# The second MLP product of a two-layer transformer kernel as three products of scaled fp16 halves

## The reference

```python
def _layer(x, wqkv, qs, ksc, wo, lg, lb, w1, b1, w2, b2):
    h = shift_token(x)
    q, k, v = jnp.split(h @ wqkv, 3, axis=-1)
    ...
    o = local_attention(q, k, v)          # windows of 128, 8 heads of 64
    x = x + o @ wo
    h = shift_token(x)
    ...
    h = (h - mu) / jnp.sqrt(var + 1e-05) * lg + lb
    h = h @ w1 + b1
    a, g = jnp.split(h, 2, axis=-1)       # 682 features each
    h = a * jax.nn.gelu(g, approximate=False)
    return x + h @ w2 + b2
```

## Time and profile before

| | |
|---|---|
| median of 3 runs | 3270.62 us (3269.76 to 3274.61) |
| profiled execution, its own time | 3271.01 us |
| profiled execution, span | 3269.2 us |
| granted TensorE clock, mean | 0.980 of full |
| TensorE matmul busy | 3107.2 us (95%) |
| VectorE busy | 2759.7 us (84%) |
| ScalarE busy | 2013.2 us (62%) |
| GpSimd busy | 1868.5 us (57%) |
| W1 products (L950) | 4224 records, 473.2 us |
| W2 products (L961) | 1536 records, 342.2 us |

### The profile page before, as it was taken

The page is one execution under the profiler, slowest core; times in us unless marked ns, Lnnn a source line. Parts: engine busy times, 40 slices in busy tenths (PEclk is TensorE's granted clock), DMA queues, the critical chain, the costliest instruction groups (busy, mean ns, idle before and its releaser), DMA issues.

```text
span 3269.2 us, 86769 instructions
## 1 busy us (share of the span) xinstructions
PE 3107.2 (95%) x25624; PEld 2611.0 (80%) x25624; DVE 2759.7 (84%) x7865; ACT 2013.2 (62%) x4509; POOL 1868.5 (57%) x2307
## 2 busy tenths in 40 slices
PE   6999999993699999999999999999999999999997
PEld 3665748483588888888888888888888888888886
DVE  6878797976688888888888888898888898888896
ACT  5526171712367777677767777677666667667674
POOL 2333434243566566666666666666666666666673
PEclk9999999995799999999999999999999999999999
DMA  1111202026111111111111111111111111111111
GB/s 36 43 54 35 67 26 72 24 64 214 30 44 42 45 39 42 47 41 44 39 44 45 43 42 39 51 47 51 49 45 48 56 47 48 51 45 47 55 50 40
DMA packets 205471, 162.56 MB, mean 50 GB/s; under 512 B 25646, under 2 KB 203282, under 8 KB 204946
## 3 DMA queue, kind: packets, MB, share of 16 engines
q1 hardware_dynamic: 205330, 161.06, 15.9%
HBM read 106.44 MB, written 54.54 MB: 49 GB/s over the span
## 4 chain that ended last, share of the span: by engine, by line
PE 67%; issue 3%; DVE 2%; ACT 1%; POOL 1%; DMA 0%; ACTq 0%; DVEq 0%; POOLq 0%; SPq 0%
PE b_ps L874 15%; PE b_ps L950 14%; PE b_ps L961 8%; PE b_ps L902 7%; PE b_ps L890 7%; PE b_ps L915 6%; PE b_ps L929 5%; PE b_ps L859 2%; PE b_ps L852 1%; PE b_ps L841 1%; PE b_ps L827 1%; ACT L1018 1%; ACT b_probs L1018 1%; POOL b_sq L1208 0%; DVE b_probs L1169 0%
## 5 line engine op out<-in xcount | busy, mean ns | idle before, releaser
L874 PE MATMUL b_ps<-b_wqkv,b_hT_hi 128*128 128x512 f32 x1536 | 495.8, 404 | 14.6 <-DVE b_qT_low L1116 13.6
L1018 ACT ACTIVATE b_probs<-b_probs,b_negmax 128x256 f32<-128x256 f32 x1024 | 505.5, 497 | 4.1 <-DVE b_negmax L1156 3.3
L950 PE MATMUL b_ps<-b_h2T,b_w 128*128 128x256 f16 x4224 | 473.2, 273 | 0.7 <-ACT b_h2T L981 0.7
L950 PEld LDWEIGHTS b_ps<-b_h2T,b_w 128*128 128x128 f16 x4224 | 414.0, 98 | 48.7 <-ACT b_h2T L981 0.8
L1208 POOL TENSOR_TENSOR b_sq<-b_sq 128x512 f32<-128x512 f32 (+5 forms) x768 | 418.2, 545 | 60.6 <-ACT b_sq L997 20.1
L1240 POOL TENSOR_TENSOR b_rn<-b_ss_min,b_mhalf 128x16 f32<-128x16 f32 x128 | 374.8, 2928 | 119.2 <-DVE b_ss_min L1068 119.0
L1169 DVE TENSOR_SCALAR b_probs<-b_probs,b_rinv 128x256 f32<-128x256 f32 x1024 | 426.8, 458 | 18.2
L1218 POOL TENSOR_TENSOR b_rstd<-b_var,b_mhalf 128x1 f32<-128x1 f32 x128 | 72.0, 562 | 571.6 <-DVE b_var L1129 571.6
L443 PE MATMUL a_ps<-a_xs,a_E 128*128 128x256 f16 x3072 | 345.2, 273 | 4.1 <-POOL a_xs L234 4.0
L874 PEld LDWEIGHTS b_ps<-b_wqkv,b_hT_hi 128*128 128x128 f32 x1536 | 282.5, 191 | 76.5 <-DVE b_qT_low L1116 18.7
L961 PE MATMUL b_ps<-b_w,b_hid 128*128 128x256 f32 x1536 | 342.2, 379 | 1.2 <-DVE b_hid L1192 1.2
(11 more groups left out here) (137 smaller groups left out, 6653.6 us busy)
## 6 DMA issues: line engine op xcount, KB each, us to landing
b_hx<-xs_dram SPq DMA_DIRECT2D x256, 64.0 KB, 1.9
b_rot<-rot_dram SPq DMA_DIRECT2D x128, 128.0 KB, 2.1
b_xr<-xs_dram SPq DMA_DIRECT2D x128, 128.0 KB, 2.1
xp_dram<-b_xp SPq DMA_DIRECT2D x128, 128.0 KB, 1.7
b_h<-xp_dram SPq DMA_DIRECT2D x256, 64.0 KB, 1.8
a_xn<-in_L_attn_x_dram SPq DMA_DIRECT2D x20, 512.0 KB, 3.8
a_x_res<-in_L_attn_x_dram SPq DMA_DIRECT2D x66, 128.0 KB, 2.1
x_dram<-a_x SPq DMA_DIRECT2D x64, 128.0 KB, 1.7
```

Of the source, the lines that this page charges most:

```text
L874: last = nc.tensor.matmul(ps[:, bank, :], hT[:, k, :], wqkv[:, ds(layer(s), 1), part, k, bank * INNER:(bank + 1) * INNER], start=(k == 0 a ...
L950: last = nc.tensor.matmul(ps[:, bank, half * 2 * P:(half + 1) * 2 * P], w1[:, ds(layer(2 * j), 1), wp, k, first:first + P], h2T[:, hp, k, ...
L1018: nc.scalar.activation(probs[:, h, :], probs[:, h, :], ACT.Exp, bias=negmax[:, h:h + 1], scale=-1.0, accum_out=rowsum[:, h:h + 1]).then_in ...
```

## The change

The W2 product is made of fp16 halves like the W1 product. Both `w2` and `hid` are scaled by powers of two and split into a high and a low half, and each fp32 product becomes three fp16 products (high by high, high by low, low by high). For `w2` this is done in the preparation; for `hid` ScalarE writes the high half in two pieces of three chunks, at the end of its even slot, and VectorE the low half in two pieces, in the odd slot after its low half of kT. The output add takes the scale out again. TensorE's W2 products wait for the low halves.

```diff
@@ phase_b, sizes and preparation
-        w2 = sb("w2", [P, LAYERS, HC, D])
+        w2 = sb("w2", [P, LAYERS, 2, HC, D], F16)
+        hid_scale, out_unit = sb("hid_scale", [P, LAYERS]), sb("out_unit", [P, LAYERS])
...
-                sp.dma_start(mask_f[:], consts["mask"].rearrange("n p j -> p n j")).then_inc(loaded, 16)
+                sp.dma_start(mask_f[:, 0, :], consts["mask"][0]).then_inc(loaded, 16)
+                sp.dma_start(mask_f[:, 1:3, :], consts["mask"][EVEN_MASK:ODD_MASK + 1].rearrange("n p j -> p n j")).then_inc(loaded, 16)
...
@@ gpsimd, preparation
-                        pool.wait_ge(top_ready, LAYERS)
+                        pool.wait_ge(top_ready, 3 * LAYERS)
...
@@ scalar, preparation
-                act.wait_ge(loaded, 16 * DMAS)
-                act.wait_ge(cleared, 4)
-                for l in range(LAYERS):
-                    nc.scalar.activation(w2[:, l], w2[:, l], ACT.Copy, scale=w1_unit[:, l:l + 1])
+                act.wait_ge(w2_scale_ready, 1)
+                for l in range(LAYERS):
+                    nc.scalar.activation(w2[:, l, 0], w2_f[:, l], ACT.Copy, scale=w2_scale[:, l:l + 1]).then_inc(w2_hi, 1)
@@ vector, preparation
+                dve.wait_ge(loaded, 16 * DMAS)
+                dve.wait_ge(cleared, 4)
+                for l in range(LAYERS):
+                    nc.vector.tensor_reduce(top[:, 1, l:l + 1], w2_f[:, l].rearrange("p c n -> p (c n)"), AX.X, ALU.max, apply_absolute_value=True).then_inc(top_ready, 1)
...
+                for l in range(LAYERS):
+                    dve.wait_ge(bias_added, l + 1)
+                    nc.vector.tensor_reduce(top[:, 2, l:l + 1], b1[:, l, :], AX.X, ALU.max, apply_absolute_value=True).then_inc(top_ready, 1)
...
                 dve.wait_ge(top_shared, 1)
...
+                dve.wait_ge(w2_scale_ready, 1)
+                for l in range(LAYERS):
+                    dve.wait_ge(w2_hi, l + 1)
+                    nc.vector.scalar_tensor_tensor(w2[:, l, 1], w2_f[:, l], w2_scale[:, l:l + 1], w2[:, l, 0], ALU.mult, ALU.subtract)
@@ tensor, odd slot
-                        pe.wait_ge(hid_ready, HC * (j + 1))
+                        pe.wait_ge(hid_lo, 2 * (j + 1))
...
                             for c in range(HC):
-                                last = nc.tensor.matmul(ps[:, 3, n * D:(n + 1) * D], hid[:, c, n * P:(n + 1) * P], w2[:, ds(layer(2 * j), 1), c, :],
-                                                        start=(c == 0), stop=(c == HC - 1))
+                                for a, (hp, wp) in enumerate(PARTS):
+                                    last = nc.tensor.matmul(ps[:, 3, n * D:(n + 1) * D], hid_hl[:, hp, c, n * P:(n + 1) * P],
+                                                            w2[:, ds(layer(2 * j), 1), wp, c, :],
+                                                            start=(c == 0 and a == 0), stop=(c == HC - 1 and a == 2))
@@ scalar, even slot, after the six gelus
+                        for part in range(2):
+                            chunks = slice(part * HC // 2, (part + 1) * HC // 2)
+                            act.wait_ge(hid_ready, HC * j + (part + 1) * HC // 2)
+                            wait(act, w2_done, j)
+                            nc.scalar.activation(hid_hl[:, 0, chunks, :], hid[:, chunks, :], ACT.Copy, scale=hid_scale[:, ds(layer(2 * j), 1)]).then_inc(hid_hi, 1)
@@ vector, layer_output
-                            nc.vector.tensor_tensor(xpp[:, n, :], ps[:, 3, n * D:(n + 1) * D], xb[:, (r - 6 + n) % 4, :], ALU.add).then_inc(xpp_ready, 1)
+                            nc.vector.scalar_tensor_tensor(xpp[:, n, :], ps[:, 3, n * D:(n + 1) * D], out_unit[:, ds(layer(2 * j), 1)], xb[:, (r - 6 + n) % 4, :],
+                                                           ALU.mult, ALU.add).then_inc(xpp_ready, 1)
@@ vector, odd slot, after the low half of kT and layer_output, before bn_stats
+                    j = pairs - 2
+                    if r % 2 == 1 and in_range(2 * j):
+                        for part in range(2):
+                            chunks = slice(part * HC // 2, (part + 1) * HC // 2)
+                            dve.wait_ge(hid_hi, 2 * j + part + 1)
+                            nc.vector.scalar_tensor_tensor(hid_hl[:, 1, chunks, :], hid[:, chunks, :], hid_scale[:, ds(layer(2 * j), 1)], hid_hl[:, 0, chunks, :],
+                                                           ALU.mult, ALU.subtract).then_inc(hid_lo, 1)
@@ vector, even slot, before the six products into hid
-                        wait(dve, w2_done, j)
+                        wait(dve, hid_hi, 2 * j)
```

More of the change, by code:

```diff
@@ L50 @@
 W1_TOP = 2.0 ** 13
+HID_TOP, PRE_FLOOR = 2.0 ** 15, 2.0 ** -50
 NT = LAYERS * NW
@@ L552, in phase_b @@
             step, scale_ready, w1_hi, bias_added = sem("step"), sem("scale_ready"), sem("w1_hi"), sem("bias_added")
+            w2_scale_ready, w2_hi = sem("w2_scale_ready"), sem("w2_hi")
             block = ctx.enter_context(nc.Block())
-            DMAS_ROT, DMAS = 1 + 6, LAYERS * 5 + 4
+            DMAS_ROT, DMAS = 1 + 6, LAYERS * 5 + 5
             @block.sync
@@ L652, in _ @@
                     dve.wait_ge(w1_gained, KD * (l + 1))
-                    nc.vector.tensor_reduce(top[:, l:l + 1], w1_f[:, l].rearrange("p k n -> p (k n)"), AX.X, ALU.max, apply_absolute_value=True).then_inc(top_ready, 1)
+                    nc.vector.tensor_reduce(top[:, 0, l:l + 1], w1_f[:, l].rearrange("p k n -> p (k n)"), AX.X, ALU.max, apply_absolute_value=True).then_inc(top_ready, 1)
+                dve.wait_ge(loaded, 16 * DMAS)
[3 more added lines that the diff above has]
+                for l in range(LAYERS):
+                    nc.vector.tensor_tensor(b1[:, l, :], ps[:, l, 0:W1_BLOCKS], b1_f[:, l, :], ALU.add).then_inc(bias_added, 1)
+                for l in range(LAYERS):
+                    dve.wait_ge(bias_added, l + 1)
+                    nc.vector.tensor_reduce(top[:, 2, l:l + 1], b1[:, l, :], AX.X, ALU.max, apply_absolute_value=True).then_inc(top_ready, 1)
+                for l in range(LAYERS):
+                    dve.wait_ge(qkv_hi, l + 1)
+                    nc.vector.tensor_tensor(wqkv[:, l, 1], wqkv_f[:, l], wqkv[:, l, 0], ALU.subtract)
+                for l in range(LAYERS):
+                    dve.wait_ge(wo_hi, l + 1)
+                    nc.vector.tensor_tensor(wo[:, l, 1], wo_f[:, l], wo[:, l, 0], ALU.subtract)
                 dve.wait_ge(top_shared, 1)
@@ new lines, in _ @@
+                dve.wait_ge(step, 5)
+                nc.vector.tensor_scalar(w1_scale[:], pow2_inv[:, 0], W1_TOP, None, ALU.mult).then_inc(scale_ready, 1)
+                nc.vector.tensor_scalar(w2_scale[:], pow2_inv[:, 1], W1_TOP, None, ALU.mult).then_inc(w2_scale_ready, 1)
+                nc.vector.scalar_tensor_tensor(pre_top[:], top_all[:, 0], float(D), top_all[:, 2], ALU.mult, ALU.add).then_inc(step, 1)
+                dve.wait_ge(step, 6)
+                nc.vector.tensor_scalar(pre_floor[:], pre_top[:], PRE_FLOOR, None, ALU.max).then_inc(step, 1)
@@ new lines, in _ @@
+                dve.wait_ge(step, 7)
+                nc.vector.tensor_scalar(pre_pow2[:].bitcast(I32), pre_floor[:].bitcast(I32), 0x7F800000, None, ALU.bitwise_and).then_inc(step, 1)
+                dve.wait_ge(step, 8)
+                nc.vector.scalar_tensor_tensor(pre_sq[:], pre_pow2[:], 4.0, pre_pow2[:], ALU.mult, ALU.mult).then_inc(step, 1)
+                dve.wait_ge(step, 9)
+                nc.vector.reciprocal(pre_inv[:], pre_sq[:]).then_inc(step, 1)
+                nc.vector.tensor_scalar(pre_half[:], pre_sq[:], 1.0 / HID_TOP, None, ALU.mult).then_inc(step, 1)
@@ L668, in _ @@
+                dve.wait_ge(step, 11)
+                nc.vector.scalar_tensor_tensor(hid_scale[:], pre_inv[:], HID_TOP, w1_unit[:], ALU.mult, ALU.mult)
+                nc.vector.tensor_tensor(out_unit[:], pre_half[:], w2_unit[:], ALU.mult)
                 dve.wait_ge(scale_ready, 1)
@@ L671, in _ @@
                     nc.vector.scalar_tensor_tensor(w1[:, l, 1], w1_f[:, l], w1_scale[:, l:l + 1], w1[:, l, 0], ALU.mult, ALU.subtract)
-                    dve.wait_ge(wo_hi, l + 1)
-                    nc.vector.tensor_tensor(wo[:, l, 1], wo_f[:, l], wo[:, l, 0], ALU.subtract)
-                dve.wait_ge(loaded, 16 * DMAS)
+                dve.wait_ge(w2_scale_ready, 1)
+                for l in range(LAYERS):
+                    dve.wait_ge(w2_hi, l + 1)
+                    nc.vector.scalar_tensor_tensor(w2[:, l, 1], w2_f[:, l], w2_scale[:, l:l + 1], w2[:, l, 0], ALU.mult, ALU.subtract)
                 nc.vector.tensor_copy(ident_h[:], ident_f[:])
-                nc.vector.tensor_copy(mask[:], mask_f[:])
+                nc.vector.tensor_copy(mask[:, 0, :], mask_f[:, 0, :])
+                nc.vector.tensor_copy(mask[:, 1:ODD_MASK, :], mask_f[:, 1:2, :].to_broadcast([P, ODD_MASK - 1, 2 * P]))
+                nc.vector.tensor_copy(mask[:, ODD_MASK, :], mask_f[:, 2, :])
                 for l in range(LAYERS):
```

(5 more changed lines are left out.)

27 lines of the change are left out of this document (14 added, 13 removed).

## The result

The changed kernel took 3457.27 us (median of 4 runs, 3454.87 to 3460.95) against 3270.19 beside it: ratio 1.057, interval 1.0552 to 1.0588. It is 187 us slower; the forecast was 3420, 149 slower, range 3340 to 3465. The profiled execution took 3454.87 us with a span of 3453.1, so 184 us more than the profiled execution of before.

A forecast was written before the change was run, and what follows sets the result against it. TensorE was taken as the bound before the change. Layer 0's 48 us, layer 1's 87 and the preparation's 14 make 149, on the profiled 3271.0: 3420 us; 3390 to 3450 by its price bounds, full range 3340 to 3465.

The forecast's parts named there:

- rival (b): More waits than counted: layer 1's loop-head gap on VectorE also comes to layer 0's 13 turns, 18 us more, 3438; chance 0.10.
- TensorE's part: W2 product: 12 fp32 products of 5.18 us become 36 fp16 products of 3.93 us, 1.25 us less per pair.
- ScalarE's and VectorE's parts: Odd slot: two copies at 0.8 us make qT 1.5 later; two subtractions at 0.9 make later VectorE work 3.3 later.
- TensorE is 1.55 late per pair: Layer 0, next slot's q product: starts at 47.6 for 46.08, saving already counted; 48 us over 31 pairs.
- The waits on TensorE: Odd slots: idle some 1.3 us before h2's transposes, 0.4 before the v product, 1.1 before next q product or kr's transposes.
- Rival (a): A probs scaling slips in ahead of kr, so hT's low half comes about 0.8 us earlier: 3370; chance 0.18.
- Layer 1: Output statistics stand in VectorE's pause, so delay is 1.2 to 1.3 larger, about 2.8 per pair: 87 us over 31 pairs.
- The gap: VectorE's 2.48 us pause at the head of layer 1's loop, once in four slots, released by nothing in the profile.
- 0.18 that was left of the pause: VectorE's pause before oT's low half, 1.36 us in layer 0; in layer 1 output statistics leave 0.18.
- never in layer 0: The prediction's reading of the profile before: VectorE's loop-head pause comes in layer 1's loop and not in layer 0's.
- The preparation: Before the second phase: waiting for loads 4.7 us, reductions 3.4, w2 low-half subtractions 3.4, tiny operations 2; taken as 14.
- Rival (c): Faster: TensorE stays the bound, odd slot's added delay is at most 1.5 us, the 80 us come through: 3205; chance 0.10.

## Why the prediction held, and which terms were off

The direction and the mechanism held: the added work stands ahead of what VectorE passes on to TensorE, and the saving on TensorE is worth nothing behind it. The number held with less right. 3457 lies above the 3390 to 3450 that the forecast gave itself; it is in the full range by what rival (b), the gap in layer 0, had added to it, and (b) had been given 0.10.

**TensorE's part** was right: 3.93 us for 36 products. That the saving is worth nothing in the sum was in its steps, where the q product is late by VectorE's delay whatever the product takes; the run with the old product kept measures 0.14 us a pair in layer 0 and nothing in layer 1 at full clock, of 1.25. My expectation for that run forgot this and put the product on the chain.

**ScalarE's and VectorE's parts** were small by a tenth: 0.88 for 0.8 a copy, so qT's low half is 1.8 late and not 1.5; 0.93 for 0.9 a low half. Together 3.7 us in place of 3.3. The working lost another 0.1 where it put the last rotation's end, 35.81 and 3.3 more, at 39.0. So the transposes of h2 are 2.15 late for 1.7, and TensorE at the next q product 1.85 for 1.55; the gap-free pair is 2.0 longer. Of the step "TensorE is 1.55 late per pair" the size is 0.4 short: layer 0 without its gap is 60 us longer, not 48. Its path is not quite the one that was followed either: at the next slot the wait that ends last in layer 0 is kr's, from GpSimd, and not that of the low half of hT.

**The waits on TensorE** came where they were said to: 1.21 before the transposes of h2 (1.3 was said), 0.5 before the v product (0.4), 0.7 before kr's transposes (1.1). Rival (a), the scaling slipping ahead of kr, happened by a hair (1458.20 against 1458.27 for kr on GpSimd). The low half of hT came 0.3 us earlier against oT's, of the 0.8 it was priced at, and that gave nothing in layer 0, where TensorE waits for kr.

**Layer 1** agrees with its term, 91 against 87, for the wrong reasons. The gap left it, 0.75 a pair less, which the forecast had only in a rival, and its pair without gaps is 3.6 longer for 2.8: 3.7 less the 0.18 that was left of the pause. I had added to an undersized 1.55. That 91 meets 87 is luck.

**The gap** is the term that was missing: the step "never in layer 0" was carried over into the forecast. In layer 0 it costs 22 us; 18 were put on it in rival (b), with the remark that by the Trainium skill's rule for blocks layer 1 could be freed. Both happened, though by blocks of another size. The gap's 22 us and the undersized links' 12 are the 34 by which layer 0 was missed (82.5 for 48), and they are as much as the whole was missed by, 184 less 149, because the rest (6 less in the start, 4 more in layer 1, 2 more at the end) cancels.

**The preparation** was 10.3 for 14, of which 8.1 are left at the first W1 products of the profiled execution, and up to 14 in others. The wait for loads (4.21 for 4.7), the reductions (3.41 for 3.4) and the low halves (3.54 for 3.4) were right; the low halves of wqkv and wo, moved ahead, ran under GpSimd's maximum, which took back the rest.

**Rival (c)**, faster, would have needed both prices under half of their rows; they were above them. Its 3205 isn't reached with the work spread out either.

The fastest kernel measured is the fp32 one with 36 idle instructions between its loops, 3253.7 us. The best one with the split is 1% above it. Whether the split can pass it stays open, and so does what the moves of hT's halves would give the fp32 kernel. Relieving VectorE without a new wait on ScalarE may be what the split needs, and the one try of that failed.

## What to carry to other kernels

When engines follow each other by 0.2 us in fixed order, price an added operation by its place in the queue: what it delays behind it, and the pause that takes this up. 1.25 us saved on the engine with the highest share was worth nothing, and placing the added 3.7 us, and hT's halves with them, where the engines had pauses was worth 158 us. Don't put an operation that waits ahead of work that others wait for, however short it is: one of 0.41 us cost 131 us here. Look at the head of each loop for a pause that nothing releases, and count the packets of the instruction queue before and after an edit: a few instructions more or less can move some 20 us from one loop to another.
